# Two recurrent layers in one loop: two products go ahead of a third on TensorE, and two additions are made four steps at a time

## The reference

```python
a = x_t @ Wx + b + h @ Wh            # layer 0, four gates of 128
c = sigmoid(a_f) * c + sigmoid(a_i) * tanh(a_g)
h = sigmoid(a_o) * tanh(c)
x1_t = x_t + h                       # layer 1's input
m = concat(x1_t, u) @ W1 + b1        # layer 1, two column blocks of 128
g = sigmoid(m_g + 1.0)
u = g * u + (1 - g) * tanh(m_c)
out_t = x1_t + u
```

## Time and profile before

| | |
|---|---|
| median of three runs | 232.16 us |
| profiled execution, its span | 228.34 us, 226.2 us |
| PE busy, weight loads busy | 221.1 us (98%), 206.6 us (91%) |
| DVE busy | 198.8 us (88%), 1555 instructions |
| ACT busy | 134.1 us (59%) |
| granted TensorE clock | 0.998 of full speed |

### The profile page before, as it was taken

The page is one execution under the profiler, slowest core; times in us unless marked ns, Lnnn a source line. Parts: engine busy times, 40 slices in busy tenths (PEclk is TensorE's granted clock), DMA queues, the critical chain, the costliest instruction groups (busy, mean ns, idle before and its releaser), DMA issues.

```text
span 226.2 us, 12499 instructions
## 1 busy us (share of the span) xinstructions
PE 221.1 (98%) x4850; PEld 206.6 (91%) x4850; DVE 198.8 (88%) x1555; ACT 134.1 (59%) x903; POOL 3.7 (2%) x12
## 2 busy tenths in 40 slices
PE   7999999999999999999999999999999999999994
PEld 5899999999999999999999999999999999999883
DVE  4889989899899898998998998989989989899895
ACT  3655666656566666665566566665666666656652
POOL 2400000000000000000000000000000000000000
PEclk9999999999999999999999999999999999999999
DMA  6000001010010001000010001101001000000000
GB/s 186 26 17 26 16 26 49 14 29 26 20 45 26 24 20 49 26 16 26 28 39 26 26 14 29 49 14 28 26 21 46 26 26 16 26 16 16 14 14 14
DMA packets 12006, 6.70 MB, mean 30 GB/s; under 512 B 1447, under 2 KB 11693, under 8 KB 11949
## 3 DMA queue, kind: packets, MB, share of 16 engines
q1 hardware_dynamic: 11376, 5.33, 8.4%
q10 hardware_dynamic: 572, 0.59, 0.7%
HBM read 3.82 MB, written 2.10 MB: 26 GB/s over the span
## 4 chain that ended last, share of the span: by engine, by line
DVE 79%; ACT 11%; issue 4%; PE 3%; DMA 1%; ACTq 0%
DVE cell_bank L574 13%; ACT act_bank L492 11%; DVE hT L581 8%; DVE pair L595 7%; DVE x1T L623 7%; DVE acts L603 7%; DVE scan_add L568 7%; DVE h_high L582 6%; DVE u_rest L609 6%; DVE outT L631 6%; DVE pair L597 6%; DVE h_low L588 6%; DMA xT<-in_x_dram 1%; PE a L291 1%; PE a L283 0%
## 5 line engine op out<-in xcount | busy, mean ns | idle before, releaser
L265 PE MATMUL gate_f<-hT,wh_raw 128*128 128x32 f32 x254 | 47.0, 267 | 0.3 <-DVE hT L581 0.2
L265 PEld LDWEIGHTS gate_f<-hT,wh_raw 128*128 128x128 f32 x254 | 37.8, 188 | 9.8 <-DVE hT L581 8.1
L473 ACT ACTIVATE gate_f<-gate_f 128x32 f32<-128x32 f32 x127 | 23.1, 182 | 34.2 <-PE gate_f L265 34.2
L492 ACT ACTIVATE act_bank<-cell_bank 128x32 f32<-128x32 f32 x128 | 23.3, 182 | 33.3 <-DVE cell_bank L574 33.2
L581 DVE TENSOR_TENSOR hT<-out_gate,act_bank 128x32 f32<-128x32 f32 x128 | 23.9, 187 | 21.0 <-ACT act_bank L492 21.0
L498 ACT ACTIVATE acts<-a 128x64 f32<-128x64 f32 x128 | 28.6, 223 | 17.8 <-PE a L291 4.6
L574 DVE TENSOR_TENSOR_SCAN cell_bank<-act_bank,scan_add 128x64 f32<-128x64 f32 x128 | 38.0, 297 | 0.1
L283 PE MATMUL a<-h_high,w1x_scaled 128*128 128x32 f16 x256 | 35.4, 177 | 0.2
L283 PE MATMUL a<-h_high,w1x_third 128*128 128x32 f16 x256 | 35.4, 177 | 0.0
L283 PE MATMUL a<-h_high,w1x_rest 128*128 128x32 f16 x256 | 35.4, 176 | 0.0
L285 PE MATMUL a<-h_low,w1x_fp 128*128 128x32 f16 x256 | 35.4, 176 | 0.0
(11 more groups left out here) (114 smaller groups left out, 1071.9 us busy)
## 6 DMA issues: line engine op xcount, KB each, us to landing
xT<-in_x_dram SPq DMA_DIRECT2D x45, 64.0 KB, 2.0
out_dram<-outT SPq DMA_DIRECT2D x32, 64.0 KB, 1.6
wx_s<-in_L_cond_Wx_dram SPq DMA_DIRECT2D x1, 256.0 KB, 2.9
wh_raw<-in_L_cond_Wh_dram ACTq DMA_DIRECT2D x1, 256.0 KB, 3.3
w_raw<-in_L_cond_weight_dram ACTq DMA_DIRECT2D x1, 256.0 KB, 3.5
xT<-in_x_dram ACTq DMA_DIRECT2D x1, 64.0 KB, 3.3
bias_rows<-in_biases_dram ACTq DMA_DIRECT2D x1, 3.0 KB
condT<-in_cond_dram SPq DMA_DIRECT2D x1, 16.0 KB, 3.2
```

Source lines behind the costliest of these rows:

```text
L265: nc.tensor.matmul(gate_step(GATE_F, j), wh_raw[:, GATE_F * P:(GATE_F + 1) * P], hT[:, (j - 1) % RING, :], start=False, stop=True, skip_gr ...
L473: return nc.scalar.activation(out, gate_step(q, j), func)
L492: nc.scalar.activation(tanh_c[:, :], cell[:, :, 1], ACT.Tanh).then_inc(tanh_c_ready, 1)
```

## The change

On PE the call of `layer1_rest` moves up: it now stands directly behind `layer1_high`, ahead of `project0`. `layer1_low` stays behind `project0`.

On DVE `add_layer0` and `add_layer1` leave their places in the middle of every step. Each is made for four steps by one instruction of 128x128, at a step's end, behind `layer1_low`: `add_layer0` at j mod 4 = 0 for the last four steps, `add_layer1` at j mod 4 = 2 for the four steps whose x1 was made two steps before. The last three steps and the last step of `out` have additions of their own behind the loop, and `add_layer0` for the last four steps stands between `layer1_pair` and `layer1_state` there. The counts that SP waits for are divided by four.

```diff
             def store(h, slot):
-                sp.wait_ge(out_ready, HS * (h + 1))
+                sp.wait_ge(out_ready, h + 1)
...
-                        sp.wait_ge(x1_ready, HS * (h + 1))
+                        sp.wait_ge(x1_ready, h + 1)
...
                             layer1_input(l)
                             layer1_high(r, l)
+                            layer1_rest(r, l)
...
                     if not (first and j < 2):
-                        layer1_rest(r, l)
                         layer1_low(r, l)
...
             def add_layer0(s, j, x_count):
                 i, slot = j % RING, j // HS
-                dve.wait_ge(h_ready, s + 1)
-                if j % HS == 0:
-                    dve.wait_ge(x_in[slot], x_count)
-                nc.vector.tensor_tensor(x1T[:, i, :], hT[:, i, :], xT[:, j * N:(j + 1) * N],
-                                        ALU.add).then_inc(x1_ready, 1)
+                dve.wait_ge(h_ready, s + HS)
+                dve.wait_ge(x_in[slot], x_count)
+                nc.vector.tensor_tensor(x1T[:, i:i + HS, :].rearrange("p t n -> p (t n)"),
+                                        hT[:, i:i + HS, :].rearrange("p t n -> p (t n)"),
+                                        xT[:, j * N:(j + HS) * N], ALU.add).then_inc(x1_ready, 1)
...
+            def add_layer1(j, steps, free):
...
+                done = nc.vector.scalar_tensor_tensor(
+                    out=outT[:, slot, o:o + steps * N],
+                    in0=acts1[:, 1, i:i + steps, :].rearrange("p t n -> p (t n)"), scalar=0.5,
+                    in1=x1T[:, i:i + steps, :].rearrange("p t n -> p (t n)"), op0=ALU.mult, op1=ALU.add)
+                if (j + steps) % HS == 0:
+                    done.then_inc(out_ready, 1)
...
                         hidden(s - 1, l0)
-                        if not (first and j == 1):
-                            add_layer0(s - 1, l0, s0 + 16 if j else s0)
                         hidden_low(s - 1, l0)
                     if layer1_runs:
                         layer1_pair(s - 2, l1)
-                    if not (first and j < 3):
-                        add_layer1(l2, s0 + 16 if j > 2 else s0)
-                    if layer1_runs:
                         layer1_state(s - 2, l1)
...
+                    if j % HS == 0 and s:
+                        add_layer0(s - HS, (j - HS) % BODY, s0 + 16 if j else s0)
+                    if j % HS == 2 and s > HS:
+                        add_layer1((j - HS - 2) % BODY, HS, s0 + 16 if j > HS else s0)
```

More of the change, by code:

```diff
@@ L619, in add_layer0 @@
                 i, slot = j % RING, j // HS
-                dve.wait_ge(h_ready, s + 1)
-                if j % HS == 0:
-                    dve.wait_ge(x_in[slot], x_count)
-                nc.vector.tensor_tensor(x1T[:, i, :], hT[:, i, :], xT[:, j * N:(j + 1) * N],
-                                        ALU.add).then_inc(x1_ready, 1)
-            def add_layer1(j, free):
-                i, slot, o = j % RING, j // HS % SLOTS, j % HS * N
-                if j % HS == 0:
-                    dve.wait_ge(out_free[slot], free)
-                nc.vector.scalar_tensor_tensor(out=outT[:, slot, o:o + N], in0=u_of(j), scalar=0.5,
-                                               in1=x1T[:, i, :], op0=ALU.mult, op1=ALU.add).then_inc(out_ready, 1)
+                dve.wait_ge(h_ready, s + HS)
[4 more added lines that the diff above has]
+            def add_layer1(j, steps, free):
+                i, slot, o = j % RING, j // HS, j % HS * N
+                if o == 0:
+                    dve.wait_ge(out_free[slot], free)
+                done = nc.vector.scalar_tensor_tensor(
[4 more added lines that the diff above has]
+                    done.then_inc(out_ready, 1)
             def body(s0, first):
@@ L636, in body @@
                     s = s0 + j
-                    l0, l1, l2 = [(j - back) % BODY for back in (1, 2, 3)]
+                    l0, l1 = [(j - back) % BODY for back in (1, 2)]
                     layer1_runs = not (first and j < 2)
@@ L661, in body @@
                         to_fp16(w1x_fp16[:, :], w1x_scaled[:, :])
-                        add_layer0(0, 0, 16)
+                    if j % HS == 0 and s:
+                        add_layer0(s - HS, (j - HS) % BODY, s0 + 16 if j else s0)
+                    if j % HS == 2 and s > HS:
+                        add_layer1((j - HS - 2) % BODY, HS, s0 + 16 if j > HS else s0)
             for s0 in range(0, T, BODY):
@@ L666, in _ @@
             hidden(T - 1, BODY - 1)
-            add_layer0(T - 1, BODY - 1, T)
             hidden_low(T - 1, BODY - 1)
             layer1_pair(T - 2, BODY - 2)
-            add_layer1(BODY - 3, T)
+            add_layer0(T - HS, BODY - HS, T)
             layer1_state(T - 2, BODY - 2)
@@ L673, in _ @@
             layer1_low(T - 2, BODY - 2)
-            add_layer1(BODY - 2, T)
+            add_layer1(BODY - HS, HS - 1, T)
             layer1_pair(T - 1, BODY - 1)
@@ L677, in _ @@
             dve.wait_ge(u_ready, T + 1)
-            add_layer1(BODY - 1, T)
+            add_layer1(BODY - 1, 1, T)
 _INS = ["x", "cond_1024", "L0_cond_Wx", "L0_cond_Wh", "biases", "L1_cond_weight"]
```

## The result

The changed kernel takes 233.24 us (median of six runs, 233.09 to 237.02); six runs of the kernel before stand at 228.18 to 232.39, median 230.25. The ratio is 1.0216, 95% interval 1.0200 to 1.0232: slower by 2.2%. That it is slower is clear; that it is slower by more than 2% is only just so. The profiled execution took 233.18 us with a span of 231.3, against 228.34 and 226.2. (The runs of most kernels here fall on two levels 3.9 us apart; from here on times and ratios are those of the lower level unless the text says otherwise.)

A forecast was written before the change was run, and what follows sets the result against it. Layer 0's dependency loop was taken as the bound, 1.68 us a step, layer 1's a little shorter. 228.34 + 5.5 (PE's order) + 0.1 (behind the loop) = 233.9 us, stated as 235.0 for two run levels; range 228 to 240.

The forecast's parts named there:

- The stated 235.0: Median stated in us, between 233.9 at the lower run level and 237.8 at the upper.
- The growth forecast per step: Layer 1's loop becomes the bound at 1.72 us: 0.045 more per step over 122 steps, 5.5 us.
- Part 1: Additions leaving the middle of DVE's step: gain of nothing, since h_low and the state wait for results 0.22 us anyway.
- The bound of 0.01 per step: Upper bound in us on the gain from removing the small additions from the middle of DVE's step.
- The price of a wide place: A 128x128 addition holds DVE's queue 0.22 us, between 0.11 for 128x32 and 0.52 for 128x384.
- The 0.1 behind the loop: Behind the loop, a wide addition replaces a small one ahead of a state instruction: 0.11 us, once.
- Part 2: PE's middle products ahead of `project0`: their 0.24 us wait for u_rest is exposed, layer 1's loop grows to 1.72 us.
- two waits: At k = 0, 1 and 3, `project0` also waits for an x chunk: 0.04 us in 5/16 of steps, 0.01.
- The covered wait: Rival, chance 0.27: without L631 the state starts 0.11 earlier, layer 0 stays the bound, 228.3 us, within 228 to 231.
- The short DVE: Rival, chance 0.07: DVE's queue is short, 0.11 us net freed per step, 14 us in all, 214 us.
- The slower case: Rival, chance 0.18: wide additions hold DVE 0.30 us, h 0.07 late in two steps of four, 238.2 us.
- the sign that the prediction gave for it: On DVE, h starting directly behind a wide addition with no idle time would show wide additions delaying h.

The follow-up runs named there:

- the narrow additions: Kernel before with only the additions moved, each only 128x32 wide, three quarters of the sums left out: 228.21 to 228.30 us, against 228.17 to 228.35 at full width.
- the wait taken away: Changed kernel with the middle products multiplying the previous step's u_rest, long ready, order and number of products kept: 227.67, 227.68 and 227.90 us.
- the four products in the changed kernel: Changed kernel with four more products of a zeroed tile in each step, behind project0: 245.29 to 245.68 us.
- two instructions on DVE: Changed kernel with two 128x32 DVE instructions, results unread, between L597 and the state: 242.94 to 243.20 us.
- one instruction on DVE: Changed kernel with one 128x32 DVE instruction, result unread, between L597 and the state: 232.43 to 232.90 us.

## Why the prediction was right

**The sum.** 233.9 us was forecast for an execution like the profiled one, and it took 233.18; +2.4% forecast, +2.2% measured. The stated 235.0 allowed for the upper level; the median came out at 233.24 because five of six runs fell on the lower one, which nothing in the prediction decides. The growth forecast per step has a slip in it: 1.72 - 1.678 is 0.042, not 0.045, and 122 x 0.042 = 5.1 us would have given 233.5.

**Part 1, the additions: nothing.** Right: alone, they give 0.9986 (0.9957 to 1.0015), no change, and the gap from L597 to the state stays 0.22 with nothing in it. The bound of 0.01 per step was right too for h_low: 104.89 - 104.68 = 0.21 against 0.22 with L623 between, a gain that shows in no step. The price of a wide place was right: where one came so late that h stood behind it, h started 56.53 - 56.32 = 0.21 after it, with the tanh over since 56.28 (the last rows of this document), against 0.22. Its start was put too late (it is 0.08 behind u_low, not 0.11), so it leaves the queue at 104.53 and has 0.04 to spare ahead of h, not 0.01. The 0.1 behind the loop came: from the last h to the end of the span are 231.3 - 226.48 = 4.82 us, and 226.2 - 221.48 = 4.72 before.

**Part 2, the order: the exposed wait.** The mechanism was right. Term by term, from the step shown above: pair to u_rest 105.65 - 105.09 = 0.56 (forecast 0.55), to the first middle product 0.24 (0.24), to `project0` 0.12 (0.12), to the low products 0.30 (0.30), to the tanh 0.25 (0.24), to the next pair 0.25 (0.25 to 0.26; 106.81 is where it starts). Sum 1.72, where I had 1.70 to 1.71 and 0.01 for the steps in which `project0` has two waits.

**The step that was mis-sized** is this last one. In step j = 9, one of the five of 16, `project0` stands 0.12 behind the first middle product (106.01 - 105.89), and it is 0.11 to 0.12 in all others: the second wait costs nothing there. The 0.01 that it was given was needed elsewhere: the other terms are each up to 0.01 longer than forecast. That the sum came out at 1.72 all the same is two small errors that cancel, and luck. The total of 122 steps with 0.041 is 5.0 us; forecast 5.5, most of the difference being the slip named above.

**The rivals.** The covered wait fell with the additions alone: freeing DVE's places doesn't bring the state forward. The short DVE fell with the same run. The slower case fell with the narrow additions. But the sign that the prediction gave for it, an h directly behind a wide addition with no idle time, did appear, in half of the steps (65 waits ahead of h where there were 127), without any loss: the addition fills DVE's idle time up to the moment when the tanh is done. A better sign is h's distance from that tanh, which stayed at 0.21. Nor did its 88% single DVE out as the engine that is short: PE's weight loads were busy 91%.

## What to carry to other kernels

Before moving an instruction ahead in an engine's written order, ask for what it waits, and what stood in front of it that covered that wait: here `project0`, 0.30 us long and ready before u_rest was, covered a result that needs 0.24 us to arrive, and after the move it stood behind it. Before freeing an engine of instructions, look at the start times with and without them: where two neighbours are 0.22 us apart either way, the filler was free. Where two loops run side by side, find the room of each (here 0.023 us of 1.68) with a dose of known length before changing the one that isn't the bound.

## What was not expected of the hardware

- The three or four microseconds between the two levels of the runs come from the start: the forget weight load takes 318 ns instead of 189 between 8 and 16 us, and with it go steps of 2.2 to 3.1 us instead of 1.7 to 2.1, behind a first h that is 1.6 us later. From about 17 us on the steps are alike (1.680 us with 8 warm-up products and with 25). The profile's own column of the granted clock (the third from the end) says 1.00 for the stretch in question, so only the durations show it. The kernel with 8 warm-up products, busy time of PE, weight loads, DVE, ACT and POOL between 8 and 16 us:

```profile
8.00:16.00 8.00, 8.00 (x93) 7.41 (x92) 4.41 (x26) 3.13 (x22) 2.10 (x4) 1.00 0.01 3
```

- In three of the kernels with the additions at a step's end (the changed one, the additions alone, the wait taken away) the one of step 28 came late, with DVE idle and nothing that the profile names as the cause: 0.2 us, once. Three others have one such step too, at another place (step 4 with the narrow additions, 16 with the four products in the changed kernel, 84 with two instructions on DVE), that with one instruction on DVE shows none behind its slow start, and no profile with the additions in the middle of the step has any. It is a small part of the measured differences, and what it waited for stays open. In the changed kernel:

```profile
55.98 0.17 DVE L614 TENSOR_TENSOR u_low<-u_rest 128x32 bf16<-128x32 f32 x1
56.32 0.29 DVE L622 TENSOR_TENSOR x1T<-hT,xT 128x128 f32<-128x128 f32 x1 [0.17 <-issue]
56.53 0.18 DVE L581 TENSOR_TENSOR hT<-out_gate,act_bank 128x32 f32<-128x32 f32 x1
```
